# One core of Trainium2: the Wu product of row tiles 3 and 7 is moved to the head of the second graph layer

## What is computed

```python
xn  = LN(x)
h   = layer_norm(xn, g, b)                      # weights g, b
o1  = gat_conv(h,  W1, heads 4 x 192)           # graph layer 1: masked softmax over neighbours
o2  = gat_conv(o1, W2, heads 2 x 96)            # graph layer 2
gnn = concat([xn, o2]) @ Wu + bu                # Wu: (768 + 192) x 768
mix = linear_attention(xn, Wq, Wk, Wv) @ Wo + bo
x   = x + gnn + mix
out = x + top2_moe(LN(x))                       # 8 experts, 768 -> 384 -> 768
```

## Time and profile before

| | us |
|---|---|
| three runs of the kernel before | 987.56, 987.81, 989.25 (median 987.81) |
| the profiled execution, its own time | 990.63 |
| its span, first to last instruction | 988.9 |
| what lies around the span in that execution (990.63 - 988.9) | 1.73 |

### The profile page before, as it was taken

The page is one execution under the profiler, slowest core; times in us unless marked ns, Lnnn a source line. Parts: engine busy times, 40 slices in busy tenths (PEclk is TensorE's granted clock), DMA queues, the critical chain, the costliest instruction groups (busy, mean ns, idle before and its releaser), DMA issues.

```text
span 988.9 us, 17421 instructions
## 1 busy us (share of the span) xinstructions
PE 921.2 (93%) x6467; PEld 679.0 (69%) x6469; DVE 753.5 (76%) x1703; ACT 355.2 (36%) x474; POOL 127.2 (13%) x147
## 2 busy tenths in 40 slices
PE   6899999999998999999999999669998799999994
PEld 6667766666655565567699999468866566666662
DVE  7888999996966787795799997799989544444442
ACT  5751121313254224323245553135547232222220
POOL 3400000000010000000000000000010245545431
PEclk9999999999999999999999999879998899999997
DMA  9611121263458384476693100044085578777850
GB/s 326 195 41 49 49 96 49 81 242 145 145 202 275 123 276 150 147 256 213 228 384 156 54 1 1 0 162 174 27 311 208 215 211 189 188 190 185 210 133 0
DMA packets 61468, 155.45 MB, mean 157 GB/s; under 512 B 11956, under 2 KB 31286, under 8 KB 58442
## 3 DMA queue, kind: packets, MB, share of 16 engines
q1 hardware_dynamic: 47034, 112.32, 32.1%
q0 software_dynamic: 9936, 34.23, 13.9%
q10 hardware_dynamic: 4416, 7.78, 2.1%
HBM read 108.34 MB, written 48.94 MB: 159 GB/s over the span
## 4 chain that ended last, share of the span: by engine, by line
PE 71%; DVE 19%; DMA 3%; issue 3%; ACT 2%; DVEq 1%; SPq 0%; POOLq 0%; ACTq 0%; POOL 0%
PE PS L1949 47%; PE PS L2238 14%; PE PS L2050 3%; DVE arena L1686 3%; DVE arena L1515 3%; DVE arena L1521 2%; PE PS L2412 2%; DVE arena L1340 1%; PE PS L2061 1%; DMA arena<-as_d 1%; PE PS L2427 1%; DVE arena L1405 1%; PE PS L2131 1%; PE PS L2118 1%; DMA arena<-in_L_ffn_bg_dram 1%
## 5 line engine op out<-in xcount | busy, mean ns | idle before, releaser
L1949 PE MATMUL PS<-arena 128*128 128x384 f16 (+7 forms) x3396 | 564.1, 322 | 6.5 <-DVE arena L1939 3.0
L1949 PEld LDWEIGHTS PS<-arena 128*128 128x128 f16 (+2 forms) x3396 | 320.0, 99 | 211.6 <-issue 11.0
L2238 PE MATMUL PS<-arena 128*128 128x193 f32 (+1 forms) x1200 | 179.5, 311 | 4.6 <-DVE arena L1521 3.9
L2238 PEld LDWEIGHTS PS<-arena 128*128 128x128 f32 x1200 | 176.6, 191 | 7.6 <-DVE arena L1521 6.2
L1119 ACT ACTIVATE arena<-arena,AS 128x1250 f32<-128x1250 f32 x60 | 80.3, 1339 | 83.9 <-DVE arena L1515 83.7
L1515 DVE SCALAR_TENSOR_TENSOR arena<-arena,AS 128x1250 f32<-128x1250 f32 x60 | 90.5, 1509 | 0.0
L1521 DVE SCALAR_TENSOR_TENSOR arena<-arena 128x1250 f32<-128x1250 f32 x60 | 87.2, 1453 | 2.7 <-PE PS L2238 2.5
L1405 DVE TENSOR_SCALAR arena<-arena 128x240 f16<-128x240 f16 x324 | 89.1, 275 | 0.0
L1404 DVE TENSOR_SCALAR arena<-arena 128x128 f16<-128x128 f16 x324 | 80.1, 247 | 0.1
L1938 DVE SCALAR_TENSOR_TENSOR arena<-PS,arena 128x768 f32<-128x768 f32 x27 | 25.8, 957 | 64.0 <-PE PS L1949 64.0
L1229 ACT ACTIVATE arena<-PS 128x1536 f16<-128x1536 f16 x27 | 39.2, 1450 | 75.1 <-PE PS L2412 75.1
(11 more groups left out here) (272 smaller groups left out, 926.7 us busy)
## 6 DMA issues: line engine op xcount, KB each, us to landing
arena<-in_L_ffn_W_dram SPq DMA_DIRECT2D x48, 384.0 KB, 3.8
fr_d<-arena SPq DMA_DIRECT2D x48, 384.0 KB, 3.0
arena<-fr_d SPq DMA_DIRECT2D x16, 1152.0 KB, 14.3
arena<-in_x_dram SPq DMA_DIRECT2D x18, 384.0 KB, 5.6
arena<-rr_d SPq DMA_DIRECT2D x4, 1280.0 KB, 8.6
g_d<-arena SPq DMA_DIRECT2D x10, 388.0 KB, 2.4
acc_d<-arena SPq DMA_DIRECT2D x10, 384.0 KB, 2.9
xf_d<-arena ACTq DMA_DIRECT2D x10, 384.0 KB, 3.2
```

What stands on the lines that cost most here:

```text
L1949: m = T.matmul(out, left[i][x], right[i][y], start=first and i + r == 0, stop=last and 3 * i + r == n - 1)
L2238: m = T.matmul(ps[sum_bank(h, b)][:, r * (C + 1):(r + 1) * (C + 1)], (PT1 if deep == 3 else PT)[i % deep][:, d * P:(d + 1) * P], feats, st ...
```

## The change

1. PE no longer makes `graph_part` for tiles 3 and 7 (LATER). For these `mixed_part` starts the accumulation itself, is split in two halves of 18 matmuls with the tile's two mask transposes before each, and waits for `acc_ready` itself.
2. SP stores the XNT columns of tiles 3 and 7 in a new DRAM tensor xl_d. Each store is 128 partitions x 12 runs of 128 16-bit numbers. They stand behind the last G load and before the mask load.
3. In layer 1 SP waits for these stores and fills slots 0 to 2 (before: 0 to 4).
4. After layer 1's last aggregate SP loads the rows into LXT (768 KB, one run of 6144 bytes in each partition). PE makes the two tiles' Wu product in the head of layer 2: four half tiles of 18 matmuls, two before `row(0)`, two between `row(1)` and `row(2)`, in PSUM banks 4, 4, 4 and 3. ACT copies each half to LATE (128x384). POOL adds both tiles to acc_d in DRAM with accumulating DMAs.
5. Slots 3 to 5 (`graphed`) are filled when the four products are done, 6 to 9 at the place of `masked`, 10 and 11 (`summed`) after POOL's additions.
6. Three pairs of semaphores are merged into one each (logits, maps), with the same waits; s_sum0_out and s_mask0_out are shared with the new DMAs and their counts shifted.

```diff
+        LATER = (3, 7)
+        LXT = reg(O_G, len(LATER) * D).bitcast(F16).rearrange("p (b r k n) -> p b r k n", b=2, r=2, k=KC)
+        LATE = v3(reg(O_G + 2560 + NP, len(LATER) * D), 2)
-        held = range(0, 5)
-        masked = range(5, 12)
+        held = range(0, 3)
+        graphed = range(3, 6)
+        masked = range(6, 10)
+        summed = range(10, 12)
...
+        def late_bank(i):
+            return 3 if i == 3 else 4
... SP
+            for b, t in enumerate(LATER):
+                sp.dma_start(rows_d[:, b], XNT[:, :, :, t * P:(t + 1) * P].rearrange("p r k n -> p (r k) n")).then_inc(late_rows, 16)
             sp.wait_ge(s_acc_psum, NT)
             sp.wait_ge(s_p_ready, EARLY)
             sp.dma_start(mask2.rearrange("p t d -> p (t d)"), mask_d).then_inc(s_mask_in, 16)
+            sp.wait_ge(late_rows, MASKS + 32)
             for u in held:
                 experts(u)
...
             sp.wait_ge(s_agg, H1 * NT)
+            sp.dma_start(LXT.rearrange("p b r k n -> p (b r k n)"), xl_d.bitcast(F16)).then_inc(late_rows, 16)
             sp.wait_ge(s_head_out, 5 * H1)
+            sp.wait_ge(s_late_psum, 2 * len(LATER))
+            for u in graphed:
+                experts(u)
             sp.wait_ge(s_max_done, (H1 + H2) * NT)
             for u in masked:
                 experts(u)
+            sp.wait_ge(late_sums, 16 * len(LATER))
+            for u in summed:
+                experts(u)
... POOL
+            pool.wait_ge(xa_out[1], XAS)
+            for b, t in enumerate(LATER):
+                pool.wait_ge(s_late_ready, 2 * (b + 1))
+                g.dma_start(acc_d[t * P:(t + 1) * P, :], LATE[:, b, :], accum_op=ALU.add).then_inc(late_sums, 16)
             pool.wait_ge(s_t2_ready, (H1 + 1) * NT)
... ACT
+                def late_out(i):
+                    b, c = divmod(i, 2)
+                    act.wait_ge(s_late_psum, i + 1)
+                    a.activation(LATE[:, b, c * HALF:(c + 1) * HALF], ps[late_bank(i)][:, 0:HALF], ACT.Copy, scale=1 / UP).then_inc(s_late_ready, 1)
+                late_out(0)
+                late_out(1)
                 row_out(0)
                 row_out(1)
+                late_out(2)
+                late_out(3)
... PE, mixed_part and the tiles
+                if t in LATER and a == 0:
+                    pe.wait_ge(s_acc_ready, t - 1)
...
-                        m = product(..., first=False, last=k == KC - 1)
+                        m = product(..., first=t in LATER and k == 0, last=k == KC - 1)
...
+                    if t in LATER:
+                        for m in ms[0:1]:
+                            mask_half(m)
+                        mixed_part(t, c0, 0, KC // 2)
+                        for m in ms[1:]:
+                            mask_half(m)
+                        mixed_part(t, c0, KC // 2, KC)
+                        continue
... PE, head of layer 2
+            def late_graph(i):
+                b, c = divmod(i, 2)
+                if i == 0:
+                    pe.wait_ge(late_rows, MASKS + 48)
+                elif i < 3:
+                    pe.wait_ge(s_late_ready, i)
+                product(ps[late_bank(i)][:, 0:HALF], [(LXT[:, b, 0, k, :], LXT[:, b, 1, k, :]) for k in range(KC)], cols(WUT, c * HALF, (c + 1) * HALF)).then_inc(s_late_psum, 1)
+            late_graph(0)
+            late_graph(1)
             row(0)
             row(1)
+            late_graph(2)
+            late_graph(3)
             row(2)
+            pe.wait_ge(s_late_ready, 2 * len(LATER))
```

More of the change, by code:

```diff
@@ L204, in gps_layer @@
         junk2 = reg(O_G + 2560, NP).bitcast(BF16).rearrange("p (a b) -> p a b", a=2)
+        LATER = (3, 7)
+        LXT = reg(O_G, len(LATER) * D).bitcast(F16).rearrange("p (b r k n) -> p b r k n", b=2, r=2, k=KC)
+        LATE = v3(reg(O_G + 2560 + NP, len(LATER) * D), 2)
+        assert len(LATER) * D <= 2560 and O_G + 2560 + NP + len(LATER) * D <= 12 * UNIT
         mask2 = reg(6 * UNIT, NT * NP // 2).bitcast(BF16).rearrange("p (a b) -> p a b", a=NT)
@@ L311, in gps_layer @@
         as_d = nc.dram_tensor("as_d", (H1 * NT * P,), F32, kind="Internal").ap()
+        xl_d = nc.dram_tensor("xl_d", (P, 2 * D), F32, kind="Internal").ap()
         rr_d = nc.dram_tensor("rr_d", (H1 * 2 * NT * P,), F32, kind="Internal").ap()
         fr_d = nc.dram_tensor("fr_d", (2 * NE, P, 2, UNIT), F16, kind="Internal").ap()
-        held = range(0, 5)
-        masked = range(5, 12)
+        held = range(0, 3)
+        graphed = range(3, 6)
+        masked = range(6, 10)
+        summed = range(10, 12)
         freed = (14,)
         late = (12, 13, 15)
-        assert sorted([*held, *masked, *freed, *late]) == list(range(2 * NE))
+        assert sorted([*held, *graphed, *masked, *summed, *freed, *late]) == list(range(2 * NE))
         NCONV = 2 * NE * NPIECE
@@ L397, in gps_layer @@
         s_gbuf0 = sem("gbuf0")
-        s_as_ready = sem("as_ready")
+        s_logits_ready = sem("logits_ready")
         s_cols_psum = sem("cols_psum")
@@ L401, in gps_layer @@
         s_cols_out = sem("cols_out")
-        s_rc_ready = sem("rc_ready")
+        s_late_psum = sem("late_psum")
         s_arow_in = sem("arow_in")
@@ L498, in gps_layer @@
         s_rank_psum = sem("rank_psum")
-        s_ohtile_ready = sem("ohtile_ready")
-        s_map_scores = sem("map_scores")
+        s_late_ready = sem("late_ready")
+        s_maps_ready = sem("maps_ready")
         s_ohslot_ready = sem("ohslot_ready")
@@ L536, in gps_layer @@
         masks_out = (s_mask0_out, s_mask1_out)
+        late_rows = masks_out[0]
+        MASKS = 16 * (NT // 2)
+        late_sums = s_sum0_out
+        SUMS = (32, 0)
         rr_in = (s_rr0_in, s_rr1_in)
@@ L792, in _ @@
             for b in range(2):
-                sp.wait_ge(sums_out[b], 16 * ((NTL + 1 - b) // 2))
+                sp.wait_ge(sums_out[b], SUMS[b] + 16 * ((NTL + 1 - b) // 2))
         @block.gpsimd
@@ L917, in sums_add @@
                 if i:
-                    pool.wait_ge(sums_out[(i - 1) % 2], 16 * ((i - 1) // 2 + 1))
+                    pool.wait_ge(sums_out[(i - 1) % 2], SUMS[(i - 1) % 2] + 16 * ((i - 1) // 2 + 1))
                 g.indirect_dma_start(out=out, out_offset=bass.IndirectOffsetOnAxis(ap=found[:, i:i + 1].bitcast(U32), axis=0),
@@ L1475, in _ @@
             V.tensor_scalar(AS2[:, :, :], AS, SLOPE, None, ALU.mult)
-            V.tensor_scalar(AS8[:, :, :], AS, 1.0 - SLOPE, None, ALU.mult).then_inc(s_as_ready, 1)
+            V.tensor_scalar(AS8[:, :, :], AS, 1.0 - SLOPE, None, ALU.mult).then_inc(s_logits_ready, 1)
             for j in range(KC):
@@ L1936, in _ @@
                 if i >= 2:
[L1937 removed]
+                    dve.wait_ge(sums_out[i % 2], SUMS[i % 2] + 16 * (i // 2))
                 link(V.scalar_tensor_tensor(yb.rearrange("p (a n) -> p a n", a=2), Y, 1 / UP, BR[:, i % BB, HID:BW].rearrange("p (a n) -> p a n", a=2), ALU.mult, ALU.add))
@@ L2164, in mixed_part @@
                     for c in range(2):
-                        m = product(ps[4 + 2 * (t % 2) + c][:, 0:HALF], zq[k:k + 1], cols(KVWO, c * HALF, (c + 1) * HALF)[k:k + 1], first=False, last=k == KC - 1)
+                        m = product(ps[4 + 2 * (t % 2) + c][:, 0:HALF], zq[k:k + 1], cols(KVWO, c * HALF, (c + 1) * HALF)[k:k + 1], first=t in LATER and k == 0, last=k == KC - 1)
                 if b == KC:
@@ L2187, in _ @@
                         pe.wait_ge(s_kvwo_ready, KC)
-                        pe.wait_ge(s_as_ready, 1)
+                        pe.wait_ge(s_logits_ready, 1)
                         T.transpose(ps[3][0:H1 * NT, 0:P], AS.rearrange("p h t -> p (h t)"), ident[:, :]).then_inc(s_cols_psum, 1)
@@ L2194, in _ @@
                     if i == NJ - 3:
-                        pe.wait_ge(s_rc_ready, 1)
+                        pe.wait_ge(s_logits_ready, 2)
                         pe.wait_ge(s_mask_ready, 2 * NT)
@@ L2399, in _ @@
             keep_warm(36, 1)
-            pe.wait_ge(s_ohtile_ready, 1)
+            pe.wait_ge(s_maps_ready, 1)
             pe.wait_ge(s_ohslot_ready, 3)
@@ L2440, in _ @@
             rows_in(0)
-            pe.wait_ge(s_map_scores, NQ)
+            pe.wait_ge(s_maps_ready, 1 + NQ)
             for k in range(NS):
```

7 lines of the change are left out of this document (4 added, 3 removed).

## The result

The median went from 989.41 us (987.38 to 991.25, 13 runs) to 980.3 us (975.3 to 986.9, 13 runs): a ratio of 0.991 (0.9893 to 0.9927), 9.1 us less. Forecast were 11.4 less and, from the median of three runs known then, 976.4. The profiled execution took 983.04 us, with a span of 981.3; forecast was 979.2.

The account below looks back on a forecast made before the run. PE bounds the mixing stage and layer 1, DVE the head of layer 2; moving PE work there gives -11.68 + 0.3 = -11.4 us, so 987.81 becomes 976.4 us (979.2 profiled); range 975.2 to 981.2, some 0.8.

Parts of the forecast that it names:

- narrow forecast: Whole kernel: a gain within 1.2 us of 11.4 us, median 976.4 us; chance 0.66.
- rival B: Head of layer 2: late product at low clock does not fit, ACT's exp slips up to 4.6 us, 981.0; chance 0.14.
- What is removed: Mixing stage: two Wu half tiles of 2.92 us each from tiles 3 and 7, 11.68 us together.
- Tile 3: Mixing stage: DVE's QT is in time by 0.6 us, hidden behind PE's next Q product; cost nothing.
- rival A: Mixing stage: DVE becomes the bound, PE waits for acc_out after both tiles, 6.5 us against 0.3, 982.6; chance 0.12.
- Tile 7: Mixing stage: DVE's QT comes 1.0 us late, PE's first denominator check loses about 0.3 us.
- The new DMAs: SP's queue: row stores take 3.8 us, at the upper end 20.7; rr_d rows still land in time, so no cost.
- Rival D: Layer 1: row stores delay rr_d rows, deciding from 20.9 us of queue time; at 41.4 us, 996.9; chance 0.03.
- POOL's accumulating DMAs: Head of layer 2: nothing taken for DVE; upper end 3.2 us if the shared port lock stretches its maxima.
- The slots: Layer 2: nine expert slots instead of seven, 10.6 MB in 28 us, filled by 690 us; cost nothing.
- The head: Head of layer 2: four late halves fit before `row(0)` and `row(2)`, covered by DVE's maxima; cost nothing.

Follow-up runs that it names:

- e5: Changed kernel plus filler matmuls at three rests of PE (near 198 us, near 319 us, head of layer 2); 974.61 us, 0.9829 to the kernel before.
- e6: Kernel before plus the same filler matmuls at the same three places as e5; 985.33 us, 0.9956 to the unfilled kernel before.
- e7: e5 with the Wu product back in the mixing stage and one matmul per late half, all new DMAs, copies and slots kept; 984.69 us, 0.9944.
- e8: e5 with 18 more row stores, to a buffer nobody reads, ahead of the mask load; 985.43 us in a single run.
- e1: The changed kernel once more, unaltered, against the kernel before on one chip; 978.27 us, ratio 0.989.
- e11: The changed kernel again, on the chip of e12, against the kernel before; 979.58 us, ratio 0.9899.
- e9: e5 with each late half product computed twice into the same bank; 984.19 us, ratio 0.9946 to the kernel before.
- e12: e5 again, unaltered, on the same chip as e11; 975.3 us, ratio 0.986 to the kernel before.

## Why the prediction was right

The prediction, faster by 11.4 us by its main mechanism, held in its mechanism and its range: 9.1, 10.65 and 9.9 us in three pairs, with times of 980.3, 978.27 and 979.58 us, and 10.7 us where both kernels were filled. The narrow forecast (within 1.2 us of 11.4) was met by one of the three pairs only, and as a time the median of 980.3 lies 3.9 above the 976.4, among the 979 to 981 that the prediction gave to rival B. Of these 3.9 us 1.6 are the kernel before, whose median rose from 987.81 to 989.41 with ten more runs. Point by point:

- **What is removed.** 11.68 us minus 0.3 for the stage, 11.4; measured 11.2 in the unfilled pair of profiles and 11.27 between e5 and e6 (134.15 against 145.42). The 0.2 us too much lie at tile 7.
- **Tile 3.** With the 1.0 us taken off by which this profile runs late already at the first acc_out, QT came at 371.64 - 1.02 = 370.62, foreseen 370.63; DVE was free at 369.9, foreseen 370.0. The margin of 0.6 us on which rival A turned was 0.7. A is out at this tile: idle PE in front of the sixth check does not appear.
- **Tile 7.** PE's check started 455.21 - 444.77 = 10.44 us earlier, 11.46 without the offset, so 0.2 us of 11.68 were lost in front of it. But the four matmuls of the check then took 0.61 us in the chain where they took 0.34 before, so the Q product behind them starts only 11.2 us earlier: 0.5 us were lost, foreseen were 0.3. DVE is the chain there, as foreseen.
- **The new DMAs.** Cost nothing, as foreseen (e7). A pair of stores holds the queue for 3.9 us by e8's issues, and its packets took 19 ns each (29175 of them, 99.3% of 16 x 35 us), the 20 ns that the prediction had borrowed from the kernel's load stage. e8's stores of 256-byte runs moved 228 GB/s on the mean, against 332 GB/s for the large rows of layer 1. The Trainium skill, DMA: Bandwidth & Descriptors, "Specifications", says that below 512 bytes transfers miss line rate, as they are read, modified and written; the lower rate agrees, the reading back itself no run here shows. Rival D's distance was right to 2 us.
- **POOL's accumulating DMAs.** 1.08 and 0.89 us long; DVE's twenty maxima and column steps beside them take 29.3 us in all profiles, before included. The port lock that the Trainium skill names (SBUF — State Buffer, "SBUF: two separate sides") is not seen.
- **The slots.** Nine slots from 651.37 on; no product of the expert stage waits for one.
- **The head: the term that was mis-sized.** The prediction took nothing for the late product, since "PE enters the stretch from dense work". That holds at full clock (e1: 0.09 us). But PE does not enter from dense work: it rests at 612 for DVE's normalised rows, and in two of three profiles of the changed kernel the clock was at its lower level before the first late half began. In the profiled execution this cost 2.4 us at the logit rows and 1.0 at the exp, in e11's 2.4 and 1.07. That the 2.4 are not the change's own is argued, not shown: the kernel before has the same rest and the same code, but its one unfilled profile took 6.6 us there. The 1.0 are rival B in small, by another way than B described: its last two halves ran at full clock, and the delay came from the slow logit rows and the slow first half, which pushed `row(0)`. B's price, argued as up to 4.6 us, is real in kind (e9) and was 1.0, 1.07 and 0.1 us in the three profiles of the changed kernel. That all three pairs still lay in the range is in part luck with the clock, as the prediction had no term for where it stands at the start of the head.
- **From 11.4 to 9.1.** Not settled. What is shown: the runs of one kernel spread over 11 us and nearly order by their mean granted clock; the gains of three pairs differ by 1.5 us among themselves; with the fillers the difference is 10.7 by medians. The profiles differ in more places than the head: the first acc_out comes between 341.37 and 346.17 us, and what follows the first aggregate of layer 2 takes 327.5 us before, 326.6 after, 324.6 in e1 and 323.2 in e11. So the head of the profiled execution explains its own span and not the median. In the profiles the filling near 198 and 319 us shows (first acc_out, above); which place brings how much of the 4.4 us was not tried apart, except for the head, whose share could not be told from zero.

## What to carry to other kernels

Work moved from a stretch that its engine bounds into one where that engine waits for another is worth its full length, provided that the waiting engine really has that slack: four half products fit under DVE's maxima, while two of them between the units of layer 2, with 0.6 us of slack each, gave 4.4 us back. Price the target stretch at both clock levels, the work of its engine ahead of the moved part included, and look for a short rest just ahead of it, as the one trace of the kernel before may happen not to show the drop. Where a change is worth 1% and the clock moves runs by as much, compare stretches inside several profiles before explaining the difference of two medians; fillers in both kernels narrow the spread but did not take the clock out here.

## What the runs showed of the hardware

- A rest of TensorE of 1.2 to 3 us amid dense work was followed by a granted clock of 0.50 to 0.6 in some executions and by 1.00 in others of the same kernel, at the same place: after's windows 614 to 618 at 0.50, e1's whole head at 1.00. Thirteen runs of one kernel ran from 975.3 us (mean granted clock 0.983) to 986.9 (0.970), some 9 us for each 0.01.
- The clock also fell without such a rest: in e12 it was 0.63 from 616 to 620 us and 0.50 from 620 to 624, with PE busy for 4.00 us of each of these windows and for 3.90 and 4.00 of the two before.
- 51 matmuls of 128x256 on constants, some 0.13 us each and 6.6 us in all, in three places where PE waits for most of that anyway, took 4.4 us off the kernel before (0.9939 to 0.9972) and 4.3 off the changed one (0.9843 to 0.9878 against 0.9874 to 0.9924).
- Stores of 256-byte runs from SBUF to DRAM, 1536 runs each, hold SP for about 1.95 us each when queued behind one another (35.15 us for 18) and cost DMA time as their packets do, 19 ns each.
